# Scores of two heads side by side in the row halves of TensorE, in the first attention of a four-part kernel

## The reference, cut to what matters

```python
qkv = inputs @ W_qkv                      # 8 batches, 512 positions, 256 features
# 32 query heads, 16 key/value heads, each of 64; two query heads share one k and v
scores = einsum('bhqd,bhkd->bhqk', q, k) / sqrt(64)
scores = scores + slope[h] * (pos_k - pos_q)
scores = where(causal, scores, -inf)
attn = softmax(scores)
out = einsum('bhqk,bhkd->bhqd', attn, v)
return out.reshape(B, S, 32 * 64) @ W_out
```

## Time and profile before

| | |
|---|---|
| median of 3 runs | 3559.1 us (3557.2 to 3559.39) |
| the profiled execution | 3555.14 us, its span 3553.4 us |
| instructions in the span | 67487 |
| the first attention in the span | from about 72 to 1596 us |
| busy in the span | PE 93%, PEld 72%, DVE 68%, ACT 62%, POOL 33% |

### The profile page before, as it was taken

The page is one execution under the profiler, slowest core; times in us unless marked ns, Lnnn a source line. Parts: engine busy times, 40 slices in busy tenths (PEclk is TensorE's granted clock), DMA queues, the critical chain, the costliest instruction groups (busy, mean ns, idle before and its releaser), DMA issues. The chain is left out here.

```text
span 3553.4 us, 67487 instructions
## 1 busy us (share of the span) xinstructions
PE 3291.3 (93%) x19106; PEld 2556.4 (72%) x19106; DVE 2433.3 (68%) x6979; ACT 2192.9 (62%) x5073; POOL 1183.5 (33%) x1818
## 2 busy tenths in 40 slices
PE   5999999999999999998999997969999964999995
PEld 4777777777777777777888884546666654888885
DVE  6888888888888888876665664546666635666665
ACT  5777777777777777775556553316656630555553
POOL 4333333333333333334333330033232102243442
PEclk9999999999999999999999998969999976999998
DMA  3222222222222222224334332111111133554545
GB/s 93 58 52 46 53 54 55 52 58 52 58 52 58 52 58 52 56 53 163 124 128 134 123 128 71 42 47 28 26 32 25 28 101 114 158 126 130 135 123 160
DMA packets 175947, 280.42 MB, mean 79 GB/s; under 512 B 32850, under 2 KB 117586, under 8 KB 175826
## 3 DMA queue, kind: packets, MB, share of 16 engines
q1 hardware_dynamic: 161234, 258.94, 25.5%
q0 software_dynamic: 14592, 19.93, 3.4%
HBM read 159.79 MB, written 41.16 MB: 57 GB/s over the span
## 5 line engine op out<-in xcount | busy, mean ns | idle before, releaser
L764 POOL TENSOR_SCALAR at_p<-at_p,at_recip 128x128 f32<-128x128 f32 (+3 forms) x1028 | 533.8, 532 | 941.5 <-DVE at_recip L903 941.5
L897 DVE CUSTOM_DVE_ANT_0 at_p<-at_s_ps,at_bias 128x128 f32<-128x128 f32 (+3 forms) x1030 | 500.6, 486 | 277.9 <-PE at_s_ps L1013 266.8
L814 ACT ACTIVATE at_p<-at_p,at_nmax 128x128 f32<-128x128 f32 (+3 forms) x1030 | 576.5, 560 | 171.9 <-DVE at_nmax L897 168.6
L1020 PE MATMUL at_t_ps<-ident,at_p 128*128 128x128 f32 x2560 | 452.2, 275 | 0.4 <-POOL at_p L764 0.4
L1012 PE MATMUL at_s_ps<-at_k_twice,at_q 128*128 128x128 f32 (+3 forms) x1030 | 373.9, 363 | 8.8 <-DVE at_nmax L897 1.2
L1837 DVE CUSTOM_DVE_ANT_0 aa_a_ps<-aa_a_ps,aa_hidden 128x128 f32<-128x128 f32 (+3 forms) x512 | 247.2, 507 | 173.7 <-PE aa_a_ps L2001 170.5
L1013 PE MATMUL at_s_ps<-at_k_twice,at_q 128*128 128x128 f32 (+3 forms) x1030 | 332.6, 323 | 0.0
L1020 PEld LDWEIGHTS at_t_ps<-ident,at_p 128*128 128x128 f32 x2560 | 305.3, 140 | 20.8 <-POOL at_p L764 0.8
L1030 PE MATMUL at_o_ps<-at_pT,at_v 128*64 128x512 f32 (+3 forms) x2064 | 306.3, 439 | 0.0
L1737 ACT ACTIVATE aa_pT<-aa_b_ps 128x512 f32<-128x512 f32 (+1 forms) x384 | 196.6, 529 | 176.1 <-PE aa_b_ps L2019 173.3
L526 DVE SCALAR_TENSOR_TENSOR nw_hl<-nw_h,nw_coef_now,nw_hh 128x512 fp32r<-128x512 f32 x192 | 150.1, 782 | 165.1 <-ACT nw_hh L454 165.1
(11 more groups left out here) (321 smaller groups left out, 8361.3 us busy)
## 6 DMA issues: line engine op xcount, KB each, us to landing
at_k_twice<-at_k_parts SPq DMA_DIRECT2D x260, 256.0 KB, 3.6
w_raw<-in_w_dram SPq DMA_DIRECT2D x57, 768.0 KB
nw_w_raw<-in_w_all_dram SPq DMA_DIRECT2D x26, 1024.0 KB, 5.0
nw_w_raw<-in_w_all_dram SPq DMA_DIRECT2D x52, 512.0 KB, 6.8
nw_xh<-xh_dram SPq DMA_DIRECT2D x10, 512.0 KB, 4.2
nw_xl<-xl_dram SPq DMA_DIRECT2D x10, 512.0 KB, 4.9
at_w_raw<-in_w_heads_dram SPq DMA_DIRECT2D x18, 256.0 KB, 4.4
nw_x<-in_x_dram SPq DMA_DIRECT2D x9, 512.0 KB, 5.9
```

The source lines that it names most:

```text
L764: pool.tensor_scalar(p, p, recip[:, u:u + 1], 1.0, ALU.mult, ALU.mult).then_inc(scaled, 1)
L814: act.activation(p_sb[:, u, 0:N], p_sb[:, u, 0:N], ACT.Exp, bias=nmax[:, u:u + 1], scale=-1.0, accum_out=total[:, u:u + 1]).then_inc(exped, 1)
L897: dve.tensor_tensor_reduce(out=p_sb[:, u, 0:N], in0=s_ps[u % 2][:, 0:N], in1=bias[:, u % 2, S - N:S], scale=1.0, scalar=BIG, op0=ALU.add, ...
L1020: ins = pe.transpose(t_ps[u % 2][:, k * P:k * P + P], p_sb[:, u, k * P:k * P + P], ident[:])
```

## The change

The high parts of both heads' q now stand in slot 0 of `qst` (head 0 in rows 0 to 63, head 1 in rows 64 to 127) and the low parts in slot 1. A score is three products of 64 rows (high q with high k, low q with high k, high q with low k), and those of head 0 and head 1 are issued in turns, one in each row half, into two banks. The call now makes both units of a block. A block of 128x128 is transposed as two pieces of 64 rows, one in each row half: the first 64 queries of both heads go to `t_ps[0]`, the last 64 to `t_ps[1]`; one count of `turned` stands for a whole stage. DVE copies out the first bank, ACT the second, as many elements as before. `take_q` and `q_rest` become one operation of 128 rows each. On DVE `turn_out` goes behind both masks (and behind `q_rest` in stage 0). On PE the waits are moved to between products: the waits for `turn_v` and `weigh` to behind the first score product of stage 0, those for the transposes ahead of the third score product, and those for the next body's q and k ahead of the last block of `weigh`.

```diff
             def take_q(count, par):
                 act.wait_ge(proj, count)
-                act.activation(qst[par][0:HD, 0, :], m_ps[1 - par][0:HD, :], ACT.Copy, scale=-HD ** -0.5)
-                act.activation(qst[par][HD:P, 1, :], m_ps[1 - par][HD:P, :], ACT.Copy, scale=-HD ** -0.5)\
-                    .then_inc(q_high, 1)
+                act.activation(qst[par][:, 0, :], m_ps[1 - par][:], ACT.Copy, scale=-HD ** -0.5).then_inc(q_high, 1)
...
-            def turn_out(n, u, par):
+            def turn_out(n, qt, par):
...
-                act.activation(pT[par][:, 1, 0:qt + 1, qt * P:N], t_ps[1][:, 0:N].rearrange("p (k q) -> p k q", q=P),
+                act.activation(pT[par][:, :, 0:qt + 1, qt * P + HD:qt * P + P], turned_half(1)[:, :, 0:qt + 1, :],
                                ACT.Copy).then_inc(odd_out, 1)
...
-                dve.scalar_tensor_tensor(out=qst[par][HD:P, 0, :], in0=m_ps[1 - par][0:HD, :], scalar=-HD ** -0.5,
-                                         in1=qst[par][0:HD, 0, :].bitcast(F32), op0=ALU.mult, op1=ALU.subtract)
-                dve.scalar_tensor_tensor(out=qst[par][0:HD, 1, :], in0=m_ps[1 - par][HD:P, :], scalar=-HD ** -0.5,
-                                         in1=qst[par][HD:P, 1, :].bitcast(F32), op0=ALU.mult, op1=ALU.subtract)\
+                dve.scalar_tensor_tensor(out=qst[par][:, 1, :], in0=m_ps[1 - par][:], scalar=-HD ** -0.5,
+                                         in1=qst[par][:, 0, :].bitcast(F32), op0=ALU.mult, op1=ALU.subtract)\
                     .then_inc(proj_out, 1)
...
                     mask(n, u)
                     invert(*soon(t, qt))
-                    turn_out(t, 2 * qt, par)
                     mask(n, u + 1)
                     if qt == 0:
                         q_rest(t + 1, 1 - par)
+                    turn_out(t, qt, par)
...
+            def score(n, par, u, between=None, late=None):
+                N = (u // 2 + 1) * P
+                at = slice(u // 2 * P, u // 2 * P + P)
+
+                pe.wait_ge(masked, n * 8 + (u + 2))
+                for i, (q, k) in enumerate([(0, 0), (1, 0), (0, 1)]):
+                    if i == 1 and between is not None:
+                        between()
+                    if i == 2 and late is not None:
+                        turnable(*late)
+                    for h in range(2):
+                        rows = slice(HD * h, HD * h + HD)
+                        ins = pe.matmul(s_ps[h][:, 0:N], qst[par][rows, q, at], k_twice[par][rows, k, 0:N],
+                                        start=(i == 0), stop=(i == 2))
+                        if i == 2:
+                            ins.then_inc(scored, 1)
+
+            def turn(qt):
+
+                for h in range(2):
+                    for k in range(qt + 1):
+                        for half in range(2):
+                            rows = slice(HD * half, HD * half + HD)
+                            ins = pe.transpose(turned_half(half)[:, h, k, :], p_sb[rows, 2 * qt + h, k * P:k * P + P],
+                                               ident[rows, rows])
+                ins.then_inc(turned, 1)
+
+            def weigh(n, par, last=None):
+
                 for k in range(TT):
+                    if k == TT - 1 and last is not None:
+                        last()
...
                     if qt == 0:
-                        turn_v(t + 1, 1 - par, v_count(t + 1) + (-2))
-                        weigh(t + (-1), 1 - par)
+                        def between():
+                            values_free(t + 1, v_count(t + 1) + (-2))
+                            turned_out(t + (-1))
+                        score(n, n_par, u, between, (t, qt))
+                    else:
+                        score(n, n_par, u, None, (t, qt))
+                    turn(qt)
+                    if qt == 0:
+                        turn_v(t + 1, 1 - par)
+                        weigh(t + (-1), 1 - par, lambda: operands(t + 1, ((half + par) * 32 + 32, 1 - par)))
```

More of the change, by code:

```diff
@@ L674, in head_attention_phase, with turned_half @@
         AHEAD0 = 6
+        def turned_half(half):
+            return t_ps[half][:].rearrange("p (h k q) -> p h k q", h=2, q=HD)
         def ahead(t, qt):
@@ L815, in exps @@
                                scale=-1.0, accum_out=total[:, u:u + 1]).then_inc(exped, 1)
-            def turn_out(n, u, par):
-                qt = u // 2
-                N = (qt + 1) * P
-                act.wait_ge(turned, n * 8 + (u + 1))
-                act.activation(pT[par][:, 1, 0:qt + 1, qt * P:N], t_ps[1][:, 0:N].rearrange("p (k q) -> p k q", q=P),
+            def turn_out(n, qt, par):
+                act.wait_ge(turned, n * TT + (qt + 1))
+                act.activation(pT[par][:, :, 0:qt + 1, qt * P + HD:qt * P + P], turned_half(1)[:, :, 0:qt + 1, :],
                                ACT.Copy).then_inc(odd_out, 1)
@@ L843, in _ @@
                         exps(n, u)
-                        turn_out(t, 2 * qt + 1, par)
+                        turn_out(t, qt, par)
                         exps(n, u + 1)
@@ L903, in invert, with turn_out @@
                 dve.reciprocal(recip[:, 2 * qt:2 * qt + 2], total[:, 2 * qt:2 * qt + 2]).then_inc(recips, 1)
[L905 to L910, removed]
+            def turn_out(n, qt, par):
+                dve.wait_ge(turned, n * TT + (qt + 1))
+                dve.tensor_copy(pT[par][:, :, 0:qt + 1, qt * P:qt * P + HD], turned_half(0)[:, :, 0:qt + 1, :])\
                     .then_inc(even_out, 1)
@@ L986, in project_kv, with turn_v @@
                 project(m_ps[par], P, b)
-            def turn_v(n, par, out):
-                pe.wait_ge(vT_out, n + 1)
-                wait_alone(pe, proj_out, out, pe_ticks)
+            def turn_v(n, par):
                 for i in range(TT):
@@ L1005, in project_out @@
                     ins.then_inc(proj, 1)
[L1007 to L1021, removed]
@@ L1023, in weigh, with values_free, turned_out, operands @@
-            def weigh(n, par):
+            def values_free(n, out):
+                pe.wait_ge(vT_out, n + 1)
+                wait_alone(pe, proj_out, out, pe_ticks)
+            def turned_out(n):
                 pe.wait_ge(even_out, n * TT + (TT + 1))
                 pe.wait_ge(odd_out, n * TT + (TT + 1))
+            def operands(n, half):
+                pe.wait_ge(proj_out, q_count(n))
+                pe.wait_ge(k_copied[half[1]], half[0])
+            def turnable(n, qt):
+                pe.wait_ge(even_out, n * TT + (qt + 1))
+                pe.wait_ge(odd_out, n * TT + (qt + 1))
+                pe.wait_ge(scaled, n * 8 + (2 * qt + 2))
@@ L1037, in body @@
                     n_par = 1 - par if u < 2 * qt else par
[L1038 to L1044, removed]
-                    if qt == 0:
-                        turn_v(t + 1, 1 - par, v_count(t + 1) + (-2))
-                        weigh(t + (-1), 1 - par)
+                    if qt == 0:
+                        def between():
[8 more added lines that the diff above has]
+                        weigh(t + (-1), 1 - par, lambda: operands(t + 1, ((half + par) * 32 + 32, 1 - par)))
                     if qt == 1:
@@ L1064, in _ @@
             project(m_ps[1], 0, 0)
-            turn_v(0, 0, 1)
+            values_free(0, 1)
+            turn_v(0, 0)
             pe.wait_ge(proj_out, 2)
@@ L1070, in _ @@
             pe.wait_ge(k_copied[0], 32)
-            for u in range(AHEAD0):
+            for u in range(0, AHEAD0, 2):
                 score(0, 0, u)
@@ L1080, in _ @@
                 body(j * B + (B - 1), j * PAIRS + (PAIRS - 1), 1, 1)
+            turned_out(KVH * B - 1)
             weigh(KVH * B - 1, 1)
```

## The result

The changed kernel takes 3565.4 us (median of 20 runs, 3561.6 to 3570.3), the kernel before 3559.0 (20 runs beside it). The ratio is 1.0021, 95% interval 1.0014 to 1.0028: slower by 0.2%, where a gain of 1.5% was forecast. The profiled execution has a span of 3565.7 us.

The account below looks back on a forecast made before the run. PE was taken to bound the kernel, 11.89 us a body. PE's work fell to 11.27, the wait for q made it 11.49; 128 x 0.40 = 51 us, plus 1 for start-up, off 3559.1 gave 3507 us, range 3462 to 3575.

Parts of the forecast that it names:

- edits at nothing: Other ACT and DVE edits and moved waits in the body cost nothing; covers hold by 0.2 to 0.5 us.
- What bounds, and PE's own work in the new body: PE sets the pace in the first attention; its work per body falls from 11.89 to 11.27 us, a gain of 0.62.
- A change of the array's shape at 0.20, or 0.09 and the open load: On PE, each change of array shape costs 0.20 us, or 0.09 plus 0.05 load into `weigh`; seven and one per body.
- Two halves run together: On PE, row halves overlap: scores 2.44 to 1.86 us a body, transposes 2.18 to 1.25, at 0.0625 a pair.
- Rivals 1 and 2: Transpose pieces don't overlap, 3652 us (chance 0.12); `fp32r` score pairs don't overlap, about 3746 us (chance 0.05).
- rival 1: Transpose pieces don't overlap, each instruction's own cost binds: body 12.6 us, time 3652; chance 0.12.
- The wait for q, now inside `weigh`: PE's last block of `weigh` waits for DVE's `q_rest`, giving back 0.2 us a body: 11.49, gain 0.40.
- The sign of being wrong that the prediction names: The prediction is wrong if a wait between products leaves PE idle in stages 1 to 3.
- Rival 4: Covers fail with dearer waits between PE's products; 0.1 us in each of four stages takes the gain: 3550 to 3570; chance 0.11.

Follow-up runs that it names:

- experiment 8: The changed kernel with the `values_free` wait asking for two counts less, and `q_rest` moved ahead of stage 0's second mask on DVE: 3474.3 us, ratio 0.9765.
- experiment 9: The kernel of experiment 8 with the transposes of stage 1 moved behind the first product of `project_kv`: 3513.9 us, ratio 0.988.
- experiment 4: The kernel of experiment 1 with the transposes undone, 128x128 again, one head to each bank: 3609.9 us, ratio 1.0139.
- experiment 3: The kernel before with only the `values_free` wait moved up to between stage 0's first and second score product: 3561.3 us, ratio 1.0007.
- experiment 1: The changed kernel with the `values_free` wait asking for two counts less, so for `k_rest` and not both `add_out`: 3482.7 us, ratio 0.978.
- experiments 1 and 2: experiment 1, and the changed kernel with the strict `values_free` wait put back just ahead of `turn_v`: 3481.7 us, ratio 0.9775.
- experiment 6: The changed kernel with scores and transposes in row halves both undone, new order and strict count kept: 3627.1 us, ratio 1.0193.
- experiment 7: The changed kernel, strict count kept, with `values_free` moved behind the two waits of `turned_out`: 3538.5 us, ratio 0.9949.

## Why the prediction was wrong

The forecast was 3507 us and faster (0.77); it came out at 3565, slower. The step that failed is the one called *edits at nothing*; the others stand in their order:

- *What bounds, and PE's own work in the new body* (11.27 us): right. With both waits out of the way the body is 11.23 (experiment 8).
- *A change of the array's shape at 0.20, or 0.09 and the open load*: right within its size. Experiment 9 gives 0.30 for two that were priced at 0.34, and the trace of the changed kernel has 0.33 (1002.57 to 1002.90) from the start of a projection's last product to the first score for 0.23 of streaming.
- *Two halves run together*, also for `fp32r`, also for pieces of 64 columns: right. Rivals 1 and 2 fell: a pair of pieces takes 0.063 and experiment 4 costs 127 us; score pairs start together, and undoing them costs 119 us with what hangs on it. The Trainium skill's figure that stood beside rival 1 (TensorE: Matmul & The Clock Gate, Back-to-back issue gap) has two cases. The 62 ns for each matmul, where the sequencer decodes in microcode, do not bind here: two pieces go in 0.063 us, 0.031 each. The floor of about 60 cycles, some 25 ns on that page, lies below 0.031, and no run here tests it.
- *The wait for q, now inside `weigh`*: the mechanism was right, the size too large. I took 0.22 us; taking it away gained 0.05 to 0.07 a body (experiment 8). `q_rest` starts 0.60 behind the second mask and not 0.73.
- *Edits at nothing*: this is the step that failed. It says of DVE in stage 3 that it "ends about when the body ends, and is needed 0.4 later". That was worked out for `turn_out`, and behind `turn_out` DVE has the second `add_out`, 0.68 us more. The count in `values_free` stands in the diff, but it was never worked out to the instruction that makes it true, although this wait was moved from behind stage 0's scores and transposes to ahead of the second score pair. Its count names `add_out`, although the data that `turn_v` needs is `k_rest`'s. Worked out, the same chain gives a stall: `add_out` ends 0.6 into the body, and the second pair is due at 0.44. With the 0.12 to the loads and 0.11 for the load (experiment 3) that is 0.39 late, and the two waits behind the blocked one, whose price was not known then, make it 0.64 of the 0.66. I read the wait by what it is for and not by what it says. The sign of being wrong that the prediction names, PE idle in stages 1 to 3, looks at the other three stages.
- *Rival 4* (covers fail together with dearer waits between products, 0.11) is the nearest to what happened, with its 3550 to 3570; that the result falls into this range is in part luck. It was put as four small losses in four stages. It was one wait in one stage, of 0.66 us, of which about 0.22 is the dear part.

So the gain did arise: 11.89 - 11.29 = 0.60 us a body once the stall is gone (experiment 1), and 0.66 with the wait for q gone too. All of it was given back in stage 0, where the stall costs 0.66 a body: 128 x 0.66 = 85 us, beside 83 measured in experiment 1.

## What to carry to other kernels

When a wait is moved to an earlier place, work out which instruction makes its count true, not what the wait is meant for: a counter shared by several steps often asks for the last of them, which cost nothing where the wait stood before. Put the wait that may block behind all others at its place, so that their own steps are worked off first. Splitting an array's work into row halves pays by the group: count the changes of shape, 0.09 us of drain and the open load each, and let all small products in a stage share one.

## What the hardware showed that I had not expected

A wait on PE that is already met costs nothing to be seen while instructions are queued ahead of it (the waits between products in experiments 1 and 2, whose bodies are as long as PE's own work), and about 0.1 us when the one before it has blocked: from the end of `add_out` to the next loads it took 0.12 us with no further wait behind (experiments 3 and 7) and 0.37 with two (the changed kernel, experiment 6); exchanging the order gave back 0.22 us a body (experiment 7).
